# The negated row of maxima written by VectorE as seven contraction rows, and another order of the slots, in a decoder layer's cross-attention

## What is computed

```python
# B=32 batches, Nq=56 queries, Nkv=1500 context rows of 96, D=128, H=16 heads of 8
q = (query @ Wq + bq).reshape(B, Nq, H, 8).transpose(0, 2, 1, 3)
k = (ctx @ Wk + bk).reshape(B, Nkv, H, 8).transpose(0, 2, 1, 3)
v = (ctx @ Wv + bv).reshape(B, Nkv, H, 8).transpose(0, 2, 1, 3)
attn = softmax(clip(einsum("bhqd,bhkd->bhqk", q, k) * 8 ** -0.5, -1e4, 1e4))
x = einsum("bhqk,bhkd->bqhd", attn, v).reshape(B, Nq, 128) @ Wo + bo
```

## Time and profile before

| | |
|---|---|
| time, median of 3 runs | 972.74 us (971.3 to 974.29) |
| profiled execution, own time | 974.64 us |
| its span, first to last instruction | 972.5 us |
| TensorE | 924.9 us busy, 95% |
| VectorE | 699.5 us, 72% |
| ScalarE | 645.9 us, 66% |
| GpSimd | 351.0 us, 36% |
| share of TensorE in the chain that ended last | 84% |

### The profile page before, as it was taken

How to read it: one execution, slowest core, us unless ns; L and a number is a source line. 1 busy time by engine, 2 the same in 40 slices (tenths; PEclk the granted TensorE clock), 3 DMA queues, 4 the chain that set the end, 5 groups by cost and what they waited for, 6 DMA issues and landing times.

```text
span 972.5 us, 28783 instructions
## 1 busy us (share of the span) xinstructions
PE 924.9 (95%) x10471; PEld 741.4 (76%) x10471; DVE 699.5 (72%) x1490; ACT 645.9 (66%) x1081; POOL 351.0 (36%) x332
## 2 busy tenths in 40 slices
PE   6777999999999999999999999999999999999995
PEld 4655777777777777777777777777777778999894
DVE  6673777767676677676767767767788857777996
ACT  4654777777777777777777777777776545445554
POOL 6452362222333333222233333332222413112992
PEclk8897999999999999999999999999999999999998
DMA  5538566666655555666666555566665201002321
GB/s 141 121 79 191 120 133 140 143 136 137 137 128 119 119 119 126 141 137 138 136 137 134 119 119 119 120 137 143 137 138 111 69 1 44 23 23 86 128 114 41
...
## 3 DMA queue, kind: packets, MB, share of 16 engines
...
## 4 chain that ended last, share of the span: by engine, by line
PE 84%; ACT 5%; DVE 4%; issue 3%; SPq 2%; POOL 1%; DMA 1%; ACTq 0%; DVEq 0%; POOLq 0%
PE psum L1592 17%; PE psum L1424 16%; PE psum L1652 13%; PE psum L1431 8%; PE psum L1436 8%; PE psum L1656 4%; ACT arena L759 3%; PE psum L1679 2%; PE psum L1692 2%; PE psum L1691 2%; PE psum L1680 2%; PE psum L1681 2%; PE psum L1693 2%; PE psum L1441 1%; SPq L396 1%
## 5 line engine op out<-in xcount | busy, mean ns | idle before, releaser
L946 DVE TENSOR_REDUCE arena<-psum 128x1 f32<-128x500 f32 x672 | 447.8, 674 | 210.1 <-PE psum L1424 206.9
L759 ACT ACTIVATE arena<-psum 125x896 f32<-125x896 f32 x384 | 347.5, 916 | 109.0 <-PE psum L1592 101.7
L1424 PE MATMUL psum<-K_hi,Q_bd 128*128 128x500 f32 x672 | 319.6, 485 | 7.0 <-DVE arena L946 4.1
L547 POOL TENSOR_TENSOR arena<-arena,K_hi 128x500 fp32r<-128x500 f32 x96 | 120.7, 1257 | 403.3 <-ACT K_hi L690 403.3
L1592 PEld LDWEIGHTS psum<-Q_st,K_st 97*125 97x125 f32 x1536 | 221.6, 189 | 42.4 <-ACT arena L759 16.6
L1592 PE MATMUL psum<-Q_st,K_st 97*125 97x224 f32 x1536 | 238.6, 278 | 6.1 <-ACT arena L759 5.6
L1652 PE MATMUL psum<-arena 125*25 125x168 f32 x3072 | 170.5, 311 | 0.2
L1424 PEld LDWEIGHTS psum<-K_hi,Q_bd 128*128 128x128 f32 x672 | 128.6, 192 | 53.3 <-issue 20.8
L813 ACT ACTIVATE K_st<-psum 128x448 fp32r<-128x448 f32 x128 | 69.8, 545 | 79.5 <-PE psum L1681 78.0
L1656 PE MATMUL psum<-arena 125*9 125x56 f32 x3072 | 117.6, 213 | 0.0
L1656 PEld LDWEIGHTS psum<-arena 125*9 125x9 f32 x3072 | 94.1, 91 | 16.6
...
## 6 DMA issues: line engine op xcount, KB each, us to landing
K_st<-K_hi SPq DMA_DIRECT2D x256, 187.5 KB, 4.8
K_st<-arena SPq DMA_DIRECT2D x128, 187.5 KB, 3.4
...
Q_st<-max_row SPq DMA_DIRECT2D x224, 0.5 KB, 1.7
...
```

The source lines that it names most:

```text
L547: g.tensor_tensor(low.bitcast(F32R), low, K_hi[:, par, n * KB:n * KB + KB].bitcast(F32), ALU.subtract).then_inc(F["keys_low"], 1)
L759: a.activation(P2[c % NP].rearrange("p (n k) -> p n k", n=2), psum[0:CK, 2 + 2 * (c % 2):4 + 2 * (c % 2), 0:HQ // 2], ACT.Exp)\
L946: v.reduce_max(mx[:, n // NB, n % NB:n % NB + 1], bank_of(n)[:, 0:KB], AX.X).then_inc(F["piece_max_taken"], 1)
L1424: mm(bank_of(n)[:, 0:KB], Q_bd[:, par].rearrange("p h q -> p (h q)")[:, 128 * (n // NB):128 * (n // NB) + 128], K_hi[:, par, (n % NB) * KB ...
```

## The change

- The row of maxima becomes seven rows. `m2x` is now the last seven of 103 columns of `m2x_wide` (the others zero), so that the transposed maxima come out on partitions 96 to 102 of bank 1. VectorE multiplies them by a block of minus ones (`minus_blocks`) and writes seven contraction rows of 896 values straight into `Q_st`: row r holds its own 128 negated maxima and zeros. `K_st` has seven rows of ones. The scores contract over 103 rows instead of 97. `load_row` with its seven DMAs for each batch, and the waits for it, are gone; the scores of chunk 0 wait for VectorE instead.
- The turn is one float32r matmul (128 columns) instead of a float32 one that shows as two instructions.
- The weighted sums stand in four groups of three chunks (slots 3, 6, 9, 11) instead of five groups of 2, 3, 3, 1 and 3 (slots 2, 5, 8, 10, 11). There are still three `P2` buffers.
- Twelve pieces of a batch are done two batches ahead instead of nine; the piece maxima have two buffers; the turn moves from between pieces 0 and 1 to between pieces 4 and 5 of the batch after.
- Projections, copies, the row maxima and the steps of 1/sum move to other slots; slots 5 and 8 hold nothing on TensorE but scores. The copy out of bank 6 moves from slot 0 to slot 1.

The diff, cut to its core:

```diff
-V_SLOTS = (9, 11, 3)
-K_SLOTS = (5, 6, 8)
-SUM_SLOT, TURN_SLOT = 0, 8
-V_COPIES = (9, 11, 3)
-K_COPIES = (4, 6, 7)
-EARLY_PIECES = {0: (9,), 1: (10,), 2: (11,), 3: (12,), 4: (14,), 6: (18,), 7: (20,), 9: (2,), 10: (4,), 11: (6,)}
-MID_PIECES = {3: (13,), 5: (15, 16), 6: (19,), 8: (0,), 9: (3,), 11: (7,)}
-LATE_PIECES = {5: (17,), 8: (1,), 10: (5,), 11: (8,)}
-OUTPUTS = {2: (0, 1), 5: (2, 3, 4), 8: (5, 6, 7), 10: (8,), 11: (9, 10, 11)}
+V_SLOTS = (7, 11, 0)
+K_SLOTS = (2, 4, 6)
+COPY_SLOT, SUM_SLOTS, SCALE_SLOT = 1, (3, 3, 4, 5), 6
+ROW_SLOT, TURN_SLOT, KEEP_SLOT = 5, 9, 6
+V_COPIES = (9, 11, 0)
+K_COPIES = (2, 4, 5)
+NEXT, BEFORE_TURN = 12, 5
+EARLY_PIECES = {2: (14,), 3: (16,), 4: (18,), 6: (0,), 7: (2,), 11: (7,)}
+MID_PIECES = {7: (3,), 11: (8, 9)}
+LATE_PIECES = {0: (12,), 1: (13,), 2: (15,), 3: (17,), 4: (19, 20), 6: (1,), 7: (4,), 9: (5,), 10: (6,), 11: (10, 11)}
+OUTPUTS = {3: ((0, 0), (0, 1), (0, 2)), 6: ((0, 3), (0, 4), (0, 5)), 9: ((0, 6), (0, 7), (0, 8)), 11: ((0, 9), (0, 10), (0, 11))}
+PROJECTIONS = sorted([(c, "values", n) for n, c in enumerate(V_SLOTS)] + [(c + 0.5, "keys", n) for n, c in enumerate(K_SLOTS)])
...
-        Q_st = sb("Q_st", [DC + 1, 2, HG, 4, S], F32R)
+        Q_st = sb("Q_st", [DC + RG, 2, HG, 4, S], F32R)
         Q_bd = sb("Q_bd", [128, 2, H, S], F32R)
-        max_row = sb("max_row", [RG, 128], F32R)
+        minus_blocks = sb("minus_blocks", [128, RG])
+        ident_r = sb("ident_r", [128, 128], F32R)
+        m2x_wide = sb("m2x_wide", [128, DC + RG], F32R)
...
-        mx = at(128, RG, NB)
+        mx = at(128, 2, RG, NB)
...
-            return [(2 if n < 9 else 1, n) for n in table.get(c, ())]
+            return [(2 if n < NEXT else 1, n) for n in table.get(c, ())]
...
         def bank_of(n):
 
-            return bank[0 if n == 0 else (n + 1) % 2]
+            return bank[(n + (n >= BEFORE_TURN) + 1 + BEFORE_TURN) % 2]
...
-            def load_row(par):
-                last_row = Q_st[DC:DC + 1, par].rearrange("a g h q -> a (g h q)")
-                for j in range(RG):
-                    sp.dma_start(last_row[:, 128 * j:128 * j + 128].bitcast(F32), max_row[j:j + 1, :].bitcast(F32)).then_inc(D_["mrow"], 16)
...
-            sp.wait_ge(F["max_row_ready"], 1 + PRIME)
-            load_row(0)
...
-                if has(b, 1):
-                    sp.wait_ge(F["max_row_ready"], b + 2 + PRIME)
-                    load_row(1 - par)
...
+            step(g.memset(minus_blocks[:], 0.0))
+            keep(minus_blocks[:], [[-1, RG]], -DC, 1, ALU.not_equal, -1.0)
+            step(g.tensor_copy(ident_r[:], ident[:]))
+            step(g.tensor_scalar(m2x_wide[:], ident[:, 0:DC + RG], 0.0, None, ALU.mult))
             pool.sem_inc(consts, 1)
...
-            step(g.memset(K_st[DC:DC + 1, 0, HG - 1].bitcast(F32), 1.0))
-            step(g.memset(K_st[DC:DC + 1, 1].rearrange("p g k -> p (g k)").bitcast(F32), 1.0))
+            step(g.memset(K_st[DC:DC + RG, 0, HG - 1].bitcast(F32), 1.0))
+            step(g.memset(K_st[DC:DC + RG, 1].rearrange("p g k -> p (g k)").bitcast(F32), 1.0))
...
-                    if c == 0 and has(b, -1):
+                    if c == COPY_SLOT and has(b, -1):
...
-                    if c == 9 and has(b, 1):
+                    if c == KEEP_SLOT and has(b, 1):
                         keep_extremes(b + 1)
...
-            def piece_max(b, n):
+            def piece_max(b, par, n):
 
                 dve.wait_ge(F["max_scores_made"], b * PIECES + n + 1 + PRIME)
-                if n == 0 and (not isinstance(b, int) or b >= 1):
-                    dve.wait_ge(F["row_max_taken"], b + PRIME)
-                v.reduce_max(mx[:, n // NB, n % NB:n % NB + 1], bank_of(n)[:, 0:KB], AX.X).then_inc(F["piece_max_taken"], 1)
-
-            def row_max(b):
+                if n == 0 and (not isinstance(b, int) or b >= 2):
+                    dve.wait_ge(F["row_max_taken"], b - 1 + PRIME)
+                v.reduce_max(mx[:, par, n // NB, n % NB:n % NB + 1], bank_of(n)[:, 0:KB], AX.X).then_inc(F["piece_max_taken"], 1)
+
+            def row_max(b, par):
 
                 dve.wait_ge(F["piece_max_taken"], (b + 1) * PIECES + PRIME)
                 if not isinstance(b, int) or b >= 1:
                     dve.wait_ge(F["max_transposed"], b + PRIME)
                     dve.wait_ge(F["extremes_kept"], b + PRIME)
-                v.reduce_max(m2x, mx, AX.X).then_inc(F["row_max_taken"], 1)
-
-            def row_out(b):
+                v.reduce_max(m2x, mx[:, par], AX.X).then_inc(F["row_max_taken"], 1)
+
+            def row_out(b, par):
 
                 dve.wait_ge(F["max_transposed"], b + 1 + PRIME)
-                if not isinstance(b, int) or b >= 1:
-                    dve.wait_ge(D_["mrow"], b * (16 * RG))
-                v.tensor_scalar(max_row[:], bank[1][0:RG, 0:128], -1.0, None, ALU.mult).then_inc(F["max_row_ready"], 1)
+                if not isinstance(b, int) or b >= 2:
+                    dve.wait_ge(F["scores_made"], (b - 1) * NC + PRIME)
+                v.tensor_tensor(Q_st[DC:DC + RG, par].rearrange("p g h q -> p (g h q)").rearrange("p (j c) -> p j c", c=128),
+                                bank[1][DC:DC + RG, 0:128].unsqueeze(1).to_broadcast([RG, RG, 128]),
+                                minus_blocks[DC:DC + RG].unsqueeze(2).to_broadcast([RG, RG, 128]), ALU.mult).then_inc(F["max_row_ready"], 1)
...
             for n in range(8, PIECES):
-                piece_max(0, n)
-            row_max(0)
-            row_out(0)
-            for n in range(3):
-                piece_max(1, n)
+                piece_max(0, 0, n)
+            row_max(0, 0)
+            for n in range(BEFORE_TURN - 1):
+                piece_max(1, 1, n)
+            row_out(0, 0)
+            for n in range(max(BEFORE_TURN - 1, 0), BEFORE_TURN + 2):
+                piece_max(1, 1, n)
             dve.wait_ge(w_ps, 2)
             v.tensor_copy(WoP[:], bank[6][:, 0:256].rearrange("p (s c) -> p s c", s=2))
             v.tensor_copy(slot_rows[:], bank[6][:, 256:256 + SLOTS - 1]).then_inc(w_ev, 1)
             dve.wait_ge(w_ev, 3)
             v.memset(bank[6], 0.0).then_inc(F["bank_cleared"], 1)
-            for n in range(3, 9):
-                piece_max(1, n)
-
-            def taken(b, c, table):
+            for n in range(BEFORE_TURN + 2, NEXT):
+                piece_max(1, 1, n)
...
-                    if c == 7 and has(b, 1):
-                        row_max(b + 1)
+                    taken(b, par, c, EARLY_PIECES)
+                    taken(b, par, c, MID_PIECES)
+                    if c == ROW_SLOT and has(b, 1):
+                        row_max(b + 1, 1 - par)
                     if c == TURN_SLOT and has(b, 1):
-                        row_out(b + 1)
+                        row_out(b + 1, 1 - par)
...
-                        if c == SUM_SLOT:
+                        if c == SUM_SLOTS[0]:
...
-                    if c == 4 and has(b, -1):
+                    if c == SCALE_SLOT and has(b, -1):
...
-                if n == 2:
+                if n == BEFORE_TURN + 1:
                     if turns:
                         pe.wait_ge(F["max_row_ready"], b + PRIME)
                 elif not (isinstance(b, int) and b == 0 and n == 0):
-                    pe.wait_ge(F["piece_max_taken"], b * PIECES + (1 if n == 1 else n - 1) + PRIME)
+                    pe.wait_ge(F["piece_max_taken"], b * PIECES + (n if n == BEFORE_TURN else n - 1) + PRIME)
                 mm(bank_of(n)[:, 0:KB], Q_bd[:, par].rearrange("p h q -> p (h q)")[:, 128 * (n // NB):128 * (n // NB) + 128],
                    K_hi[:, par, (n % NB) * KB:(n % NB) * KB + KB], start=True, stop=True).then_inc(F["max_scores_made"], 1)
...
-            def turn(b):
+            def turn(b, more):
 
                 pe.wait_ge(F["row_max_taken"], b + 1 + PRIME)
-                mm(bank[1][0:RG, 0:128], m2x, ident[:], start=True, stop=True).then_inc(F["max_transposed"], 1)
+                if more and BEFORE_TURN > 1:
+                    pe.wait_ge(F["piece_max_taken"], (b + 1) * PIECES + BEFORE_TURN - 1 + PRIME)
+                mm(bank[1][0:DC + RG, 0:128], m2x_wide[:], ident_r[:], start=True, stop=True).then_inc(F["max_transposed"], 1)
 
...
-            pieces1(0)
-            turn(0)
-            pieces1(1)
+            pieces1(*range(BEFORE_TURN))
+            turn(0, True)
+            pieces1(BEFORE_TURN)
...
-            pieces1(2, 3)
+            pieces1(*range(BEFORE_TURN + 1, BEFORE_TURN + 3))
             pe.wait_ge(F["keys_copied"], 2 * NB + PRIME)
             value_project(1, 0)
-            pieces1(4, 5, 6, 7)
+            pieces1(*range(BEFORE_TURN + 3, NEXT - 1))
             pe.wait_ge(F["values_copied"], NB + 1 + PRIME)
             value_project(1, 1)
-            pieces1(8)
+            pieces1(NEXT - 1)
+
+            def bank_free(b, kind, n):
+
+                if isinstance(b, int) and b == B - 2:
+                    pe.wait_ge(F["keys_copied"], B * NB + PRIME)
```

(29 more changed lines are left out.)

35 lines of the change are left out of this document (16 added, 19 removed).

## The result

The changed kernel takes 947.95 us (median of 4 runs, 947.26 to 952.67) against 972.33 of the kernel before beside it: a ratio of 0.976, 95% interval 0.973 to 0.9789. The forecast was 948.8 us. The run that was profiled is the longest of the four, 952.67 us with a span of 950.6.

What follows compares the result with a forecast made beforehand. TensorE's order of instructions was taken to set the time. Periods -20.3, the last two batches -2.0 and the start -1.6 made -23.9 us, giving a median of 948.8 us, range 942 to 961 (chance 0.60).

Steps and rivals of the forecast that it cites:

- Group: Weighted sums on TensorE: a group costs 0.30 us whatever its length, so five becoming four saves 0.30 a period.
- Stall: Slot 2: the scores of chunk 2 wait 0.34 us for chunk 0's exponential; longer slots 0 and 1 remove it.
- Turn: Transposing the maxima on TensorE: 0.19 us becomes at most 0.11 as a single pass, 0.08 less a period.
- Bunching: VectorE's 14 piece maxima crowded into slots 11 to 4 just fit with two banks; 0.02 us a period lost.
- Rival 1: Thin places (late maxima, chunk 8's exponential) give back half the gain: 0.3 left a period, 960.4 us; chance 0.18.
- Rival 4: Group's saving belongs to lone chunk 8's surroundings, stall moves to scores 3; only turn and start left: 970 us; chance 0.03.
- Rival 3: A better start: batch 0's stall too short for the clock to fall, thin places hold: 944 us; chance 0.10.
- The row's write: VectorE's `row_out` from PSUM over 896 columns, at slot 9's group: takes 1.10 us, has 1.8 of cover, costs 0.
- Rival 2: GpSimd's spread of queries holds the wide `row_out` to 2.8 us each period: slower than before, 986 us; chance 0.09.
- 29 periods from batch 1 on: Every period from batch 1 on, 29 of them, gets 0.70 us shorter: -20.3 us.
- The last two batches: Less group, piece stall and turn there, 1.3 us, and three pieces fewer, 0.7: -2.0 us.
- The start: Without row copies SyncE's low halves come 3.1 us earlier, batch 0 stalls about 3.5; batch 1 at 100.35: -1.6 us.

Runs made afterwards that it cites:

- e1: The changed kernel with chunk 8's weighted sums in a group of their own in slot 10, five groups instead of four: 961.72 us, ratio to before 0.9882.
- e3: The new order of pieces, projections and groups with the old row (float32 maxima turn, seven DMAs, 97 contraction rows): 964.76 us, ratio to before 0.9916.
- e5: The kernel before with the third value projection and its copy moved from slot 3 to slot 0: 971.52 us, ratio to before 0.9983.
- e7: The changed kernel with VectorE's three output-projection additions in periods 28 and 29 moved to slots 0, 1 and 11: 948.74 us, ratio to before 0.9761.
- e2: The kernel before with only the new row (seven contraction rows, float32r turn, no row DMAs), order and slots as before: 966.18 us, ratio to before 0.9921.
- e4: The changed kernel with VectorE writing the row twice, one behind the other: 973.72 us, ratio to before 1.0009.
- Experiment 6: The changed kernel with GpSimd's split of the first expert's weights waiting until VectorE has scaled the second quarter's rows: 946.05 us, ratio to before 0.9722.
- e11: The changed kernel itself, run again unaltered as the measure beside later experiments: 949.15 us, ratio to before 0.976.
- Experiment 8: The changed kernel with VectorE's maximum of piece 4 taken before the first write of the row, ahead of the periods: 951.08 us, ratio to before 0.9767.

## Why the forecast was right, and where not

**The periods.** Forecast 0.70 a period, measured 0.83 over 27 of them, 22.4 us instead of 18.9. Group: 0.30 against 0.33. Stall: 0.34 against 0.34 (scores 1 to scores 2 in 0.67). Turn: 0.08 against 0.12 to 0.13. Its term was sized as if a pass could not be cheaper than 0.11; it costs 0.06. The Trainium skill ("TensorE: Matmul & The Clock Gate", Step-by-step) counts weight loads by columns; the turn's load of 103 columns has 170 to 245 ns in this trace and does not show in the starts, as the forecast assumed. Bunching: 0.02 against nothing in the loop; a maximum that is two pieces behind is always there in time. These make 0.80; the last 0.03 has no row of its own. Group and turn were tested alone (e1; the 0.12 of e3); the stall's share is read from the starts, since e5 did not bring it. Rival 1 (thin places give half back) and Rival 4 (the cost of a group belongs to its surroundings) fall with these rows and with e1. Rival 3, whose start is 3 us ahead of the forecast's 100.35, fits no median, but its start does occur: batch 1 at 96.64 in e7, with the changed kernel's prologue.

**The row's write.** 1.10 us forecast, 1.097 measured, cover 1.8 forecast, 1.75 measured. The step from 128 to 448 to 896 columns held. Rival 2, that GpSimd would hold it, falls: 1096 to 1098 ns in 32 executions. The spread of queries that it feared does not meet the row's write in the loop: it ends before (in one period at 457.86, where the write begins at 458.44), and only two of the 32 run beside an operation of GpSimd on two tensors. The trace of e2 decides it: there 31 of 32 ran 0.6 to 1.1 us beside such operations, and all took 1096 to 1098 ns. What e4 adds is how thin this is: 0.65 us are left, and 1.1 us more on VectorE at this one place cost the whole gain, though VectorE idles for 4.8 us of each period (575.93 - 445.68, over 27).

**Periods 28 and 29: missed.** The forecast took 29 equal periods. The step that failed is "29 periods from batch 1 on": the earlier trace rows showed 22.05 us for one of them before, nearly the same as its neighbours, and I read that as the same limit. VectorE already had 1.8 us more there, hidden under the old period. With a period of 21.2 it was no longer hidden: 1.4 us of the forecast, 1.7 at the measured rate, did not come. Moving the three operations to VectorE's gaps brought both periods back to 21.2 and 21.35.

**The last two batches: -2.0 forecast, +0.4 measured.** Period 30 gave 1.5. From batch 31 on the run is 1.9 longer: 3.3 more ahead of the experts and, by the luck of the profile, 1.4 less in them. The step that failed is that the gain there was summed from TensorE's steps alone (group, stall, turn, pieces). Without the row's copies in SyncE's queue the weights came earlier, and GpSimd's block of 4.6 us with them, onto VectorE's scaling. Experiment 6 shows that the block holds the scaling and costs 4.0 us there. That the removed copies brought it forward is read from the profiles of before, e2, e3 and e5, and not tested by itself. In the old order the hold costs less: in e5 the four operations took 4.60 us, and the way to the first matmul of the experts 19.26 instead of 17.63. Experiment 6 also shows what Rival 2 had right: something can hold VectorE for microseconds. It was only the wrong operation. The scaling reads and writes SBUF alone, the row's write reads PSUM.

**The start: -1.6 forecast; 0.0 in the profiled run, -3.4 in e11's, -5.3 in e7's.** The step on SyncE's queue was right: without the seven in front, the low halves of the queries go out as soon as they are ready (SP's queue, e11), and the key copy runs at 81.87, where the forecast had 81.7:

```profile
63.07 9.06 SPq L395 DMA_DIRECT2D arena<-OS_all  x12
72.17 0.59 SPq L396 DMA_DIRECT2D x_rows<-x_all  x1
72.80 4.70 SPq L378 DMA_DIRECT2D K_st<-arena  x4
```

In the first profile the first of these rows stands at 66.28 and the key copy at 84.86, no earlier than before (84.83).

A part of that is the change's own, and here a step failed that the forecast put at nothing: "GpSimd's four more constants lie ahead of its first work, which waits for VectorE." They delay not GpSimd's work but VectorE's. GpSimd's long memset of `K_st` moves from 12.38 to 13.81, and a small operation of VectorE (line 885, 0.17 us elsewhere) ends only when the memset does, with all that stands behind it (before, then after):

```profile
12.38 5.09 POOL L495 MEMSET K_st<- 1x6000 f32 x1
13.98 3.52 DVE L885 TENSOR_SCALAR arena<-arena 112x4 f32<-112x4 f32 x1
```
```profile
13.81 5.09 POOL L495 MEMSET K_st<- 7x6000 f32 x1
14.46 4.47 DVE L885 TENSOR_SCALAR arena<-arena 112x4 f32<-112x4 f32 x1
```

So GpSimd's next work begins at 26.27 instead of 24.84, in ten of the eleven profiles with the new row; in e3 and e5, with the old row, the memset stands where it stood before. In e7 line 885 got in just ahead of the memset (at 13.78), that work began at 23.39, and batch 1 at 96.64, the earliest of all that share the prologue. How much of the 1.4 us reaches batch 1 was not tested. Between the first profile and e11's, which share that delay, 2.0 of the 3.2 us at SyncE's row above arise between 40 and 52 us; from 40 to 45 the granted clock was 0.50 in the one and 0.85 in the other.

The step on TensorE was wrong: it had batch 0 at 72 and a stall of 3.5 us. Batch 0 started at 79.45 (75.89 in e11), with no stall: VectorE wrote the row ahead of the maximum that piece 5 needed, a wait of 1.90 us, and TensorE went at half clock. Experiment 8 put TensorE on the forecast's course, and batch 1 started no earlier for it. Where the term's sum comes near a profile, that is luck and not its working.

**The sum.** Forecast -23.9 against the profiled execution, measured -22.0 there and -24.4 by the medians. The periods gave 3.5 us more than forecast, the ends 3.9 less (1.5 + 2.4), the start between 1.6 less and 1.8 more (by e11): errors of both signs that nearly cancelled. The mechanism of the period was right; that the sum came within 2 us owes something to luck.
